# A decoder block on one core: the second half of its scan over ten steps instead of eleven

## What is computed

```python
x = layernorm(x + L0_attn(x))          # conv, gated delta rule, Wo, gated MLP
x = layernorm(x + L0_xattn(x, ctx))    # 16 heads of 16, softmax over 120 keys
x = layernorm(x + L0_ffn(x))           # 8 experts, the one with the largest logit
```

```python
S = a * S
pred = einsum('bhkv,bhk->bhv', S, k)
S = S + k[..., :, None] * (b * (v - pred))[..., None, :]
o = einsum('bhkv,bhk->bhv', S, q)
```

## Time and profile before

| | us |
|---|---|
| median of 3 runs | 1915.34 |
| lowest, highest | 1914.19, 1918.46 |
| profiled execution, its own time | 1919.56 |
| its span, first to last instruction | 1917.4 |
| middle phase, scan of block 1 (from 520.2 to 1013.8) | 493.6 |
| middle phase, behind the scan (to 1367.7) | 353.9 |

### The profile page before, as it was taken

One profiled execution on the slowest core, in us unless ns is written; L12 is line 12 of the kernel. 1 busy time (PEld: TensorE's weight loads), 2 busy tenths in 40 slices (PEclk: granted clock), 3 DMA queues, 4 the chain that ended last, 5 costly groups with the idle time before them and its releaser, 6 DMA issues. The chain is left out here.

```text
span 1917.4 us, 28138 instructions
## 1 busy us (share of the span) xinstructions
PE 1369.9 (71%) x6660; PEld 939.9 (49%) x6661; DVE 1199.3 (63%) x3351; ACT 756.6 (39%) x2416; POOL 1007.4 (53%) x1246
## 2 busy tenths in 40 slices
PE   6514558500047667668757999996599999999997
PEld 4413446400035555556546677775355555555554
DVE  4499999999988999999772235344232323222222
ACT  5521225401123766667864688885111111111110
POOL 3258998886679998898666323421111111121211
PEclk9857779855578888888967999997799999999999
DMA  4601114600221011110102112223311401501200
GB/s 123 210 26 34 45 34 142 234 23 0 78 66 32 22 32 39 32 32 17 37 17 88 54 38 63 100 71 123 109 49 62 164 20 37 182 30 62 67 17 6
DMA packets 97684, 125.40 MB, mean 65 GB/s; under 512 B 10001, under 2 KB 74952, under 8 KB 95560
## 3 DMA queue, kind: packets, MB, share of 16 engines
q1 hardware_dynamic: 60040, 97.22, 15.7%
q10 hardware_dynamic: 33136, 18.58, 3.3%
q0 software_dynamic: 4432, 8.73, 1.3%
HBM read 89.68 MB, written 35.74 MB: 65 GB/s over the span
## 5 line engine op out<-in xcount | busy, mean ns | idle before, releaser
L239 POOL TENSOR_TENSOR wt<-wt 128x1024 f32<-128x1024 f32 x128 | 301.5, 2356 | 46.7 <-DVE wt L184 31.9
L245 POOL TENSOR_TENSOR wt<-wt 128x512 f32<-128x512 f32 (+2 forms) x384 | 307.2, 800 | 30.1
L1868 PE MATMUL e_ph<-wt,e_g 128*128 x624 | 274.3, 592 | 0.0
L184 DVE SCALAR_TENSOR_TENSOR wt<-wt,scan 128x256 f32<-128x256 f32 x512 | 241.5, 472 | 1.8 <-POOL wt L239 1.7
L163 DVE TENSOR_REDUCE wt<-wt 128x16 f32<-128x272 f32 x512 | 218.8, 427 | 0.1
L174 DVE TENSOR_TENSOR scan<-wt,scan 128x256 f32<-128x256 f32 x512 | 214.7, 419 | 0.3
L152 DVE TENSOR_TENSOR wt<-wt,scan 128x256 f32<-128x256 f32 x512 | 209.6, 409 | 0.5 <-PEq L262 0.5
L1359 ACT ACTIVATE wt<-p_pX,p_mx 128x120 f32<-128x120 f32 x512 | 176.9, 389 | 75.0 <-DVE p_mx L1146 74.9
L1761 POOL TENSOR_TENSOR e_ve<-e_mv,eps 128x1 f32<-128x1 f32 x39 | 7.5, 191 | 368.7 <-DVE e_mv L1812 368.7
L1491 PE MATMUL p_pm<-p_w_mix,p_oT 128*128 128x256 f32 x128 | 43.9, 502 | 197.8 <-DMA p_oT<-o 168.1
L1868 PEld LDWEIGHTS e_ph<-wt,e_g 128*128 128x128 f32 x624 | 115.5, 190 | 130.8 <-issue 130.8
(11 more groups left out here) (223 smaller groups left out, 2879.4 us busy)
## 6 DMA issues: line engine op xcount, KB each, us to landing
wt<-in_L_ffn_W SPq DMA_DIRECT2D x24, 1024.0 KB
qkv<-f_st ACTq DMA_DIRECT2D x48, 256.0 KB, 2.3
p_kE<-kE SPq DMA_DIRECT2D x16, 480.0 KB, 3.6
p_vP<-vP SPq DMA_DIRECT2D x16, 480.0 KB
wt<-qkv SPq DMA_DIRECT2D x6, 1024.0 KB, 9.5
e_xt<-routed ACTq DMA_DIRECT2D x39, 130.0 KB
f_xt<-in_x SPq DMA_DIRECT2D x16, 256.0 KB, 2.9
p_oT<-o SPq DMA_DIRECT2D x16, 256.0 KB
```

Of the source, the lines that this page charges most:

```text
L184: nc.vector.scalar_tensor_tensor(s["S"][:, h, u], s["S"][:, h, (u - 1) % R], s["gate"][:, jb, h, 2, bass.ds(c * R + u, 1)], s["outer"][:], ...
L239: nc.gpsimd.tensor_tensor(x, s["S"][:, h, z * Q:(z + 1) * Q], s["qn"][:, h, z * Q:(z + 1) * Q].rearrange("p t (o d) -> p t o d", o=1).to_b ...
L245: nc.gpsimd.tensor_tensor(x[:, :, :, 0:half], x[:, :, :, 0:half], x[:, :, :, half:2 * half], ALU.add).then_inc(s["o_fold"][h], 1)
L1868: ins = nc.tensor.matmul(ph2[:], g1[:, c // (C1 // 2), c % (C1 // 2)], wt[:, bass.ds(at_b + (W2_AT + c * F2), F2)], start=(c == 0), stop=( ...
```

## The change

`PLAN` becomes ten steps, with two chunks in step 0, one in steps 1 to 4 and two in steps 5 to 9; the sum stays 16. `AGAIN` becomes 10: the second block's first pair takes stage a in step 10, while the first block's last pair is at stage c there. The phase has 23 steps. Tokens are spread evenly over the 16 places: token n of L goes to place 16n // L. With 16 or 8 tokens these are the places of before; the 12 tokens of step 0 go to places 0, 1, 2, 4, 5, 6, 8, 9, 10, 12, 13, 14. The steps between the two blocks are now, by their stages: 8 bfcde, 9 fcde, 10 acde, 11 abde, 12 abfe, 13 abfc. They were 8 bfcde, 9 fcde, 10 cde, 11 ade, 12 abe, 13 abf, 14 abfc. In step 12, f and e are on without d, so `count` for that case moves on TensorE from between `mix` and gate/up to ahead of `down`.

```diff
-    PLAN = (1, 1, 1, 2, 2, 2, 2, 2, 1, 1, 1)
-    AGAIN = M + 3
+    PLAN = (2, 1, 1, 1, 1, 2, 2, 2, 2, 2)
+    AGAIN = M + 2
...
                 def scan(i):
 
-                    if len(turns) < 2 * R:
-                        if i % 2 or i // 2 >= len(turns):
-                            return
-                        i //= 2
-                    x, u = turns[i]
-                    scan_step(nc, dve, s, 1, x, u, last=isinstance(x, int) and x == CHUNKS - 1)
+                    for n, (x, u) in enumerate(turns):
+                        if 2 * R * n // len(turns) == i:
+                            scan_step(nc, dve, s, 1, x, u, last=isinstance(x, int) and x == CHUNKS - 1)
...
+                if "e" in on and "d" not in on:
+                    pe.wait_ge(x2T_out, e + 1)
+                    count(e)
                 if "f" in on:
...
-                if "e" in on and "d" not in on:
-                    pe.wait_ge(x2T_out, e + 1)
-                    count(e)
                 if "b" in on:
```

## The result

The changed kernel takes 1941.11 us (median of 4 runs, 1939.53 to 1946.9) against 1914.76 (4 runs, 1913.39 to 1918.46): 1.014 times the time, 95% interval 1.0114 to 1.0166. The forecast was 1933 in a range of 1921 to 1942. The profiled execution took 1939.53 us, with a span of 1937.4 (was 1917.4). So the two profiles differ by 20.0 us and the medians by 26.3. What follows is read from the profiles, each of which shows one execution.

The account below looks back on a forecast made before the run. VectorE's scan was taken to bound two-chunk steps, a chain through several engines, chiefly ScalarE's, one-chunk steps. The terms sum to +17.8 on the profiled 1919.56 us; carried to the median 1915.34, that gives 1933, range 1921 to 1942.

Parts of the forecast that it names:

- Start, +14.4: Before the first pair's scores: eight more tokens cost +24.0 us, less VectorE stalls they cover; together +14.4.
- Steps 3 and 4, -18.7: One chunk instead of two: ScalarE's chain plus 2.7 for stage a gives 47.0 us each, 94.0 for 112.7.
- Steps 5 to 7. Unchanged: two chunks, 0: Middle steps of the scan keep two chunks, so their time was to stay the same: 0 us.
- Steps 8 and 9: Two chunks instead of one: VectorE's pace of 57.6 us, +1.5 and +13.1 on the intervals up to pair 6.
- p6 to p7, +8.0: Interval between the first score maxima of the first block's last two pairs: 51.6 us instead of 43.6.
- kE, +8.5: Last pair's kE load queues on SyncE behind the output store and oT load, delaying its scores: +8.5 us, bounds 6 and 15.
- Behind p7, -9.0: Last pair's maximum to the second block's first down projection: 58.5 us, including 1.6 for a lower clock, instead of 67.5.
- 1 (kE hidden): kE's load for the last pair is hidden anyway; about 1925 us, chance 0.15.
- 2 (GpSimd becomes the bound): Steps 8 and 9: eight more readouts make GpSimd hold up VectorE and the last store; about 1940 us, chance 0.13.
- 3 (the tail does not shrink): After the last pair, down waits for count and gate/up, so the -9.0 falls away or turns; 1942 us, chance 0.09.
- 4 (one-chunk steps at VectorE's pace): Steps 3 and 4 take 33 us each, 28 less than in the sum; 1905 us, chance 0.07.
- 5 (losses and gains cancel): Whole kernel: the change does nothing, 1915 us, if steps 3 and 4 come to 38 and kE is free; chance 0.06.

Follow-up runs that it names:

- experiment 6: Changed kernel with step 0's 12 tokens at the first 12 of the 16 places, not spread: 1947.54 us, ratio 1.0167.
- experiment 4: Normalising of probabilities moved from ScalarE to VectorE: changed kernel, pair 0 and half of pair 1, 1936.13 us; kernel before, last three pairs, 1920.4 us.
- experiment 1: Small semaphore instructions at the head of VectorE's program shift its loop: 77 in the changed kernel, 1934.0 us; 51 in the kernel before, 1922.6 us.
- experiment 7: Changed kernel with VectorE's loop moved by 74 small instructions, kE loaded before the store, first three normalisations and the last pair's on VectorE: 1925.67 us.
- experiment 5: Changed kernel with one-chunk steps back at the scan's end: kE first and 46 small instructions, 1925.16 us; late entry and kE in its old place, 1930.43 us.
- experiment 2: Changed kernel with kE's load moved ahead of stage a's store and loads in SyncE's program: 1938.5 us, ratio 1.0115.

## Why the prediction was right, and where it was not

**Start, +14.4: measured +12.7.** The stall ahead of the first residual is gone, as said, and the even spread costs nothing: without it the start is dearer (experiment 6). VectorE's wait for the first MLP output is 4.02, where 4.7 was left standing. But this pair of profiles is a lucky one. From the scan's first instruction in the phase to p0 the three kernels with the old start took 88.5 to 90.7 us and the eight with the new one 104.2 to 105.8, with a wait of 5.6 in seven of these eight: 15.9 on average. So the size is 14 to 17, and up to 3 us of what the medians have more than the profiles may lie here.

**Steps 3 and 4, -18.7: measured -21.1** (43.8 and 47.7 for 47 each). That a one-chunk step waits for ScalarE's chain is shown by experiment 4 for the first of them only. The added 2.7 for stage a was too much for the first of them.

**"Steps 5 to 7. Unchanged: two chunks, 0": measured +6.2.** This is the step that failed. I took the same work for the same time. The intervals p2 to p4 were 117.5 and became 123.7. Of the 6.2, 4.7 are the two gaps of 2.35 and 2.33 at the loop's turn, in which VectorE waits for its own instructions. The trace shows 8 KB packets of instructions at the gaps, and experiment 1 makes and removes them in both kernels. The Trainium skill ("Runtime: NRT & Kernel Launch", instruction fetch mechanics) says that a taken branch whose target lies outside the pages held on the chip forces a fetch of the target. By that rule a loop pays at each turn, or does not, by where it lies; the trace agrees, with 2.35 us a turn.

The other 0.7 a step (59.4 with the gaps removed, against 58.7) is read from rows; no experiment was made for it. VectorE and GpSimd in order of time, after:

```profile
750.26 1.30 DVE L1174 TENSOR_SCALAR p_x<-p_x 128x2 f32<-128x2 f32 x1
```

```profile
749.17 2.36 POOL L239 TENSOR_TENSOR wt<-wt 128x1024 f32<-128x1024 f32 x1 [0.25 <-POOL wt L223]
```

An operation on 128x2 elements lasts until GpSimd's long one ends (751.56 and 751.53). In the same step before it took 0.67 us, and in experiment 7, whose step is 58.2, it took 0.16 (row below). The same holds in all twelve kernels: wherever it takes more than 0.3 us, up to p7, it ends 0.01 to 0.04 us behind an instruction of GpSimd. The two kernels of experiment 5, which have the same plan, took 60.4 and 58.2 from p1 to p2, and this operation 2.33 and 0.16.

```profile
745.36 0.16 DVE L1180 TENSOR_SCALAR p_x<-p_x 128x2 f32<-128x2 f32 x1
```

**Steps 8 and 9.** p4 to p5 +2.9 (forecast +1.5), p5 to p6 +13.5 (forecast +13.1): VectorE's pace, as said.

**p6 to p7, +8.0, and kE, +8.5: measured +15.9 for the 16.5.** The mechanism is in the rows: store at 1004.91, oT at 1008.80, kE at 1009.22, scores at 1013.39. The forecast's +8.5 is 16.4 less 8.0, that is 8.4. The readout's end was estimated at +7.0 behind the scan's end, with the 6.4 that no row gave, and came at +4.1 (1000.8 to 1004.9), while the scan ended 5 us later than the 996 of the sum. The price is 6.1 at p7 by experiment 2, but only some 2 to 5 of it reach the end.

**Behind p7, -9.0: measured -12.3** (55.2 instead of 58.5). The wait for count is there, 1.71 ahead of it. The other profiles of kernels with the early entry and kE behind the store have 53.0 to 54.4 here. The mix took 1.97 and not the slow 3.76, so up to the down projection the 1.6 for the clock was not needed: the granted clock was 0.67 between 956 and 1001 and 1.00, the upper level (2.4 GHz), from 1050.8 to 1056. The 1.6 came one step further on, in the down projection itself. Its 24 matmuls took 7.58 us instead of the 6.00 of the earlier trace rows:

```profile
1070.59 7.58 PE L1509 MATMUL p_py<-p_wd,p_prod 128*128 128x256 f32 x24 [0.27 <-DVE total L1204]
```

The stretches of this projection (columns as in the table by stretch), first after, then before:

```profile
1070.50:1074.00 3.50, 3.41 (x9) 2.76 (x10) 0.41 (x4) 0.00 (x0) 1.90 (x2) 0.53 0.13 43
1074.00:1078.10 4.10, 4.10 (x17) 2.57 (x15) 0.00 (x0) 0.00 (x0) 0.14 (x1) 1.00 0.09 32
```

```profile
1052.80:1058.80 6.00, 6.00 (x25) 4.26 (x25) 0.00 (x0) 0.00 (x0) 0.00 (x0) 1.00 0.01 3
```

For 3.5 us the granted clock was 0.53, close to the lower level (1.2 GHz), after TensorE had waited 1.71 us for the choice and 0.27 for the positions. In the kernel before, the projection runs at the upper level throughout, behind gate and up matmuls and a wait of 1.73. The Trainium skill ("TensorE: Matmul & The Clock Gate", part 1, what's actually happening) has the clock fall after idling and return after sustained work; the trace agrees in sign here. The 5 us that I had put to it, without a row, did not appear; the 1.6 did.

**The sum.** +12.7, -21.1, +6.2, +2.9, +13.5, +15.9 and -12.3 make +17.8 at the down projection, the very sum of the prediction. That is luck in part: 8.0 us that I had not counted (6.2 in the loop, 1.4 and 0.4 in the two steps behind it) stand against 8.0 by which the start, the one-chunk steps, the way to p7 and the tail came out better. Behind it come 1.6 to p8's maximum, which the clock costs in the down projection, and 0.6 to the end, 20.0 in the span. The other 6.3 of the 26.3 are the choice of executions: the profiled one of before was 4.8 above its median, that of after 1.6 below. The median of 1941.1 lies 8 above the forecast and 0.9 below the range's upper end, so the time itself was met only narrowly.

**The rivals.** 1 (kE hidden) fell: the wait is there, though part of it is absorbed later. 2 (GpSimd becomes the bound) fell for steps 8 and 9: VectorE is busy 58.44 of 59 us and 57.22 of 58, and GpSimd lengthens its steps only by the small operation above. 3 (the tail does not shrink) fell, it shrank by 12.3. 4 (one-chunk steps at VectorE's pace) fell: 43.8 and 47.7, together 91.5, against the 76 that made the sum zero; 39.2 is the best that experiment 4 reached for one of them. 5 (losses and gains cancel) fell with the interval of the ratio. What decided is what the prediction named: a chunk is taken from steps that need it least and given to steps that pay for it in full.

The clock also answers why the kernel of experiment 7 loses 2.5 us between the down projection and p8's maximum. Its stretch of the down projection:

```profile
1052.80:1061.20 8.40, 8.38 (x24) 5.81 (x24) 0.34 (x3) 0.00 (x0) 2.03 (x2) 0.69 0.10 34
```

The 24 matmuls take 8.4 us instead of 6.0 at a granted clock of 0.69. From the down projection to p8's maximum it is 24.9 in the five kernels with the late entry and 26.3 to 27.4 in the seven with the early one. What was not tried is an order of TensorE's work that keeps this wait from standing right ahead of the down projection.

## What to carry to other kernels

Moving work out of a step pays only if its engine sets that step's length: here two steps got 21 us shorter, while the start and the last steps of the scan got 45 us longer (12.7 + 2.9 + 13.5 + 15.9), and the tail gave back only 12. Before counting on an end that comes earlier, follow the last store and load behind it; the scan ended up to 31 us earlier, and the second block's down projection came at best 1.4 us earlier. And when work ahead of a loop changes its number of instructions, look at the loop's turns for idle time with no releaser and at the count of instruction packets: "unchanged" work had become 6 us longer, 4.7 of them by these gaps.

## What the runs showed that I had not expected

A turn of VectorE's loop costs 2.31 to 2.60 us or at most 0.24, by where the loop's code lies: 51 or 77 small instructions ahead of it decide, and the packet count of the instruction queue (56, or 45 to 48) tells which.

A small operation with one tensor operand on VectorE (128x2) took 0.13 to 2.33 us, the long ones ending with the GpSimd operation that ran beside it. The Trainium skill ("GPSIMD Engine Reference", key points) says that GpSimd shares its interfaces to SBUF with VectorE, with contention for VectorE's instructions in a two-port mode or with two inputs in SBUF. The trace agrees that this operation is held up beside GpSimd; in which mode it runs no row shows. VectorE's large two-input operations (128x256) took 0.35 to 0.43 us in the two-chunk steps of this trace, whatever GpSimd did. They do not test the rule, since one of their inputs, the tile `scan`, lies in PSUM.
